# Mixture layers: the norm taken with tokens as partitions, the router on raw columns, one softmax for all tokens

## What is computed

```python
x = x + 0.5 * ffn(layernorm(x))          # two blocks of local attention and a gated MLP
x = x + ssm(layernorm(x))
x = x + 0.5 * ffn(layernorm(x))
x = x + 0.5 * mixture(layernorm(x))      # 8 experts, top 2
x = x + unit(layernorm(x))               # gated unit
x = x + 0.5 * mixture(layernorm(x))      # the same weights

def mixture(xf):
    probs = softmax(xf @ w_router)               # [tokens, 8]
    topk_w, topk_idx = top_k(probs, 2)           # not renormalised
    h = gelu(xf @ w1[e] + b1[e])                 # 128 -> 512
    return sum(topk_w * (h @ w2[e] + b2[e]))     # over the two experts
```

## Time and profile before

| | us |
|---|---|
| median of 3 runs (lowest, highest) | 1194.48 (1188.43, 1200.24) |
| the profiled execution, its own time | 1189.11 |
| its span | 1187.3 |
| mean granted TensorE clock | 0.926 of full |
| busy in the span: PE, DVE, ACT, POOL | 1012.3, 720.2, 688.2, 524.8 |
| DMA moved | 120.02 MB |

### The profile page before, as it was taken

One profiled execution on the slowest core, in us unless ns is written; L12 is line 12 of the kernel. 1 busy time (PEld: TensorE's weight loads), 2 busy tenths in 40 slices (PEclk: granted clock), 3 DMA queues, 4 the chain that ended last, 5 costly groups with the idle time before them and its releaser, 6 DMA issues.

```text
span 1187.3 us, 25908 instructions
## 1 busy us (share of the span) xinstructions
PE 1012.3 (85%) x9070; PEld 632.4 (53%) x9070; DVE 720.2 (61%) x1625; ACT 688.2 (58%) x1301; POOL 524.8 (44%) x405
## 2 busy tenths in 40 slices
PE   4788999999998876799999999999639968746995
PEld 1345555555555364355555555555339964325995
DVE  0577678777776653677776776876564423654441
ACT  2566686686673662676677667656316636623661
POOL 2664456556441542545444344433345530263451
PEclk9899999999999967999999999999759989857997
DMA  9895344455433600545444344432312240011223
GB/s 349 250 298 157 86 102 109 97 120 116 100 93 81 71 1 2 126 109 121 96 107 96 89 107 109 101 80 77 143 44 68 67 114 1 19 43 48 64 65 120
DMA packets 88511, 120.02 MB, mean 101 GB/s; under 512 B 20064, under 2 KB 72032, under 8 KB 87488
## 3 DMA queue, kind: packets, MB, share of 16 engines
q1 hardware_dynamic: 81824, 96.30, 33.8%
q0 software_dynamic: 6272, 20.44, 4.7%
q10 hardware_dynamic: 288, 1.63, 0.3%
HBM read 62.66 MB, written 22.11 MB: 71 GB/s over the span
## 4 chain that ended last, share of the span: by engine, by line
PE 65%; ACT 14%; issue 7%; DMA 6%; DVE 5%; POOL 1%; SPq 1%; ACTq 0%; DVEq 0%; POOLq 0%
PE banks L591 7%; PE banks L944 6%; PE banks L954 6%; PE banks L676 5%; PE banks L662 5%; PE banks L620 3%; PE banks L751 3%; PE banks L669 3%; PE banks L637 3%; PE banks L721 3%; PE banks L726 2%; PE banks L645 2%; DMA rstd<-arena 2%; ACT arena L1194 2%; ACT arena L1189 2%
## 5 line engine op out<-in xcount | busy, mean ns | idle before, releaser
L2041 POOL TENSOR_TENSOR arena<-arena 128x1024 f32<-128x1024 f32 x64 | 150.9, 2357 | 321.0 <-DVE arena L1644 318.7
L2030 POOL TENSOR_TENSOR arena<-arena 128x1024 f32<-128x1024 f32 x64 | 150.8, 2357 | 41.6 <-ACT arena L1189 41.6
L1636 DVE TENSOR_REDUCE arena<-banks 128x4 f32<-128x512 f32 x128 | 82.5, 686 | 93.5 <-PE banks L620 93.3
L1181 ACT ACTIVATE arena<-banks,arena 128x512 f32<-128x512 f32 x128 | 80.5, 679 | 93.6 <-PE banks L669 93.2
L591 PE MATMUL banks<-arena 128*128 128x512 f32 x256 | 128.6, 627 | 6.7 <-DVE arena L1563 5.9
L2020 POOL DMA_INDIRECT moe_outs<-arena x78 | 81.5, 1045 | 100.7 <-DVE arena L1882 88.6
L1386 ACT ACTIVATE arena<-banks,arena 128x128 f32<-128x128 f32 x312 | 89.0, 369 | 59.0 <-PE banks L944 58.9
L2013 POOL DMA_INDIRECT moe_rows<-arena x64 | 63.1, 986 | 118.5 <-DVE arena L1617 101.1
L1644 DVE TENSOR_TENSOR arena<-arena 128x1024 f32<-128x1024 f32 x64 | 78.1, 1220 | 28.4 <-DMA arena<-arena 28.4
L1194 ACT ACTIVATE arena<-banks 128x1024 f32<-128x1024 f32 x64 | 65.6, 1025 | 46.1 <-PE banks L591 45.1
L954 PE MATMUL banks<-arena 128*128 x624 | 87.5, 283 | 4.6 <-ACT arena L1386 4.4
(11 more groups left out here) (221 smaller groups left out, 1951.6 us busy)
## 6 DMA issues: line engine op xcount, KB each, us to landing
arena<-arena SPq DMA_DIRECT2D x256, 128.0 KB, 3.8
arena<-rstd SPq DMA_DIRECT2D x128, 256.0 KB, 4.3
moe_rows<-arena POOLq DMA_DIRECT2D x12, 903.0 KB, 6.6
arena<-moe_rows SPq DMA_DIRECT2D x78, 64.5 KB
arena<-in_rot SPq DMA_DIRECT2D x4, 1024.0 KB, 11.6
arena<-in_mw SPq DMA_DIRECT2D x2, 2048.0 KB, 10.8
arena<-moe_outs SPq DMA_DIRECT2D x16, 256.0 KB, 4.9
arena<-ssm_a SPq DMA_DIRECT2D x4, 512.0 KB, 6.6
```

The costliest lines, as they stand in the source:

```text
L1636: nc.vector.tensor_reduce(mx[:, e], by_row(bank[3 + e][:]), AX.X, ALU.max).then_inc(s_max, 1)
L2030: nc.gpsimd.tensor_tensor(TA[:, n % 2], RAW, ROTV[:, :, 0, c * C:(c + 1) * C], ALU.mult).then_inc(cos_done, 1)
L2041: nc.gpsimd.tensor_tensor(TA[:, n % 2], TA[:, n % 2], TB, ALU.add).then_inc(rot_sum, 1)
```

## The change

It alters both mixtures, nothing of their experts' loops but the source of the gates, and no DMA of SP.

- The weights of the router are centred once (`centred_router`: one product of 128x8 on PE, a copy on DVE into WRC, semaphore `wrc`). It stands on PE in the loop's last pass (s = 32) of the second ffn, ahead of the first piece of the mixture, and with it the wait for `moe_s_in` >= 48. DVE's copy stands behind `normalise(31)`.
- `token_rows` (PE): the rows come as four products of X's tile with the centring matrix, tokens as partitions; the products `centred` and `variance` over features, ACT's square and full-width ln and exp, DVE's multiply and the transposes go.
- `route` (PE): four router products from X and WRC. `pick` (DVE): the eight largest raw logits and their places straight from PSUM, the cast and the one-hot tables: 5 chained steps where `route` had 10.
- `moments` (DVE): four `bn_stats` and four `bn_aggr` of 128 columns, mean and variance of every token. `tokens` (ACT): ln and exp of 128x4, four copies of 128x128 with the row's scale, and a copy of the chunk from SBUF to SBUF.
- The gates: exp((logit - largest) * scale), its sum and reciprocal for all 16 tiles at once: `gates_start` behind `tile_map`, `gates_exp` on ACT, `gates_end` behind the weights of the first two tiles.
- The order of all pieces changes. In the tail of the ffn chunk 2 now comes ahead of `mlp_output(7)`; `rank(0, 0)` stands ahead of the last transposed scores; the second mixture's chunk 1 is made ahead of the unit's last silus.

The diff, cut to the new functions and the new orders:

```diff
+            def centred_router():
+                pe.wait_ge(moe_s_in, 48)
+                mm(bank[1][:, 0:NE], centre, WR, start=True, stop=True).then_inc(wrc, 1)
+
+            def route(moe, c):
+                pe.wait_ge(wrc, 2)
                 for t in range(TILES):
                     at = c * C + t * P
-                    last = mm(bank[MX_VAR[moe][c]][:, t * NE:(t + 1) * NE], YB[:, at:at + P], WR, start=True, stop=True)
+                    last = mm(bank[MX_RANK[moe][c]][:, t * NE:(t + 1) * NE], X[:, at:at + P], WRC, start=True, stop=True)
                 last.then_inc(router_mm, 1)
+
+            def token_rows(moe, c):
                 for t in range(TILES):
                     at = c * C + t * P
-                    last = nc.tensor.transpose(bank[MX_CEN[moe][c]][:, t * P:(t + 1) * P], YB[:, at:at + P], ident)
+                    last = mm(bank[MX_TOK[moe][c]][:, t * P:(t + 1) * P], X[:, at:at + P], centre, start=True, stop=True)
                 last.then_inc(xtok_mm, 1)
...
                     elif run:
                         pe.wait_ge(copied, 2 * n)
+                        pe.wait_ge(sq_done, n)
+                        centred_router()
                         pe.wait_ge(x_ffn, NCH + 1)
-                        centred(X, 0, MX_CEN[0][0])
+                        token_rows(0, 0)
...
                 if run:
-                    variance(mix, 0, MX_VAR[0][0])
+                    route(0, 0)
                 transpose_out(29, n - 3, s)
                 masks(31, n - 1)
                 values(30, n - 2, 0)
                 scores(31, n - 1)
                 values(30, n - 2, 1)
                 if run:
-                    pe.wait_ge(moe_s_in, 48)
-                    route(mix, 0, 0)
+                    rank(0, 0)
                 transpose_scores(31, n - 1)
                 hidden(6, s, 0)
...
                     pe.wait_ge(x_ffn, NCH + 2)
-                    centred(X, 1, MX_CEN[0][1])
+                    token_rows(0, 1)
+                    route(0, 1)
...
                 transpose_out(31, n - 1, s, 0)
-                if run:
-                    rank(0, 0)
                 output(7, s)
                 hidden(6, s, 1)
+                if run:
+                    rank(0, 1)
                 last_centred()
...
                 last_hidden(2)
-                if not run:
+                if run:
+                    pe.wait_ge(xtok_done, 3)
+                    pe.wait_ge(rank_dve, 2 * RANK_STEPS)
+                    pe.wait_ge(x_ffn, NCH + 3)
+                    token_rows(0, 2)
+                    route(0, 2)
...
                 mlp_output(7, s)
```

The unit's part on PE, `enter(c)` being `token_rows(1, c)` and `route(1, c)` behind their waits (x_unit; from chunk 1 on the first copy of the rows of the chunk before):

```diff
                 unit_centred(3)
-                mix_centred(0)
-                mix_variance(0)
                 down(1)
+                enter(0)
                 unit_variance(3)
-                route(mix, 1, 0)
                 up(2, range(3))
-                mix_centred(1)
                 rank(1, 0)
-                mix_variance(1)
+                enter(1)
                 up(2, range(3, 4))
                 up(3)
-                route(mix, 1, 1)
+                rank(1, 1)
                 down(2)
                 down(3)
-                rank(1, 1)
-                mix_centred(2)
-                mix_variance(2)
-                route(mix, 1, 2)
-                mix_centred(3)
+                enter(2)
+                enter(3)
                 rank(1, 2)
-                mix_variance(3)
-                route(mix, 1, 3)
                 rank(1, 3)
```

More of the change, by code:

```diff
@@ L1300, in ffn @@
                 if run:
-                    act.wait_ge(rs_out, 16 * n)
-                    act.wait_ge(unit_done, n)
-                    norm_root(mix, 1, MX_VAR[0][1])
+                    tokens(0, 1)
                 else:
@@ L1310, in ffn @@
                 if run:
-                    tokens(0, 1)
+                    tokens(0, 2)
                 else:
@@ L1598, in route @@
-                chained(TT(OH[:, tt], each, IDXF[:, tt, 0:2].unsqueeze(3).to_broadcast([P, TILES, 2, NE]), ALU.is_equal), route_dve)
-                chained(TT(MINE[:, tt], OH[:, tt, 0], OH[:, tt, 1], ALU.add), route_dve)
-                assert n[0] == ROUTE_STEPS * (k + 1)
+                for t in range(TILES):
+                    last = nc.vector.max(TOPL[:, c * TILES + t], part(moe, c, 0)[:, t])
+                chained(last, pick_dve)
+                for t in range(TILES):
+                    at = c * TILES + t
+                    last = nc.vector.max_index(TOPI[:, at], TOPL[:, at], part(moe, c, 0)[:, t])
@@ new lines, in pick, with moments @@
+                chained(last, pick_dve)
+                chained(nc.vector.tensor_copy(IDXF[:, tt], TOPI[:, tt]), pick_dve)
+                each = expert_id.unsqueeze(1).unsqueeze(1).to_broadcast([P, TILES, 2, NE])
+                chained(TT(OH[:, tt], each, IDXF[:, tt, 0:2].unsqueeze(3).to_broadcast([P, TILES, 2, NE]), ALU.is_equal), pick_dve)
+                chained(TT(MINE[:, tt], OH[:, tt, 0], OH[:, tt, 1], ALU.add), pick_dve)
+                assert n[0] == PICK_STEPS * (k + 1)
+            def moments(moe, c):
+                k = NCH * moe + c
+                dve.wait_ge(xtok_mm, k + 1)
+                for t in range(TILES):
+                    last = nc.vector.bn_stats(PART[:, c * TILES + t], bank[MX_TOK[moe][c]][:, t * P:(t + 1) * P])
+                last.then_inc(tok_dve, 1)
+                dve.wait_ge(tok_dve, 2 * k + 1)
+                for t in range(TILES):
+                    last = nc.vector.bn_aggr(MOMENT[:, c * TILES + t], PART[:, c * TILES + t])
+                last.then_inc(tok_dve, 1)
@@ L1751, in ffn @@
                 if run:
-                    norm_chunks(mix, first_plain, [0])
+                    dve.wait_ge(cos_done, n)
+                    centred_router()
+                    moments(0, 0)
                 maximum(n - 1)
                 subtract(n - 1)
+                if run:
+                    pick(0, 0)
                 divide(n - 2)
-                if run:
-                    dve.wait_ge(cos_done, n)
-                    route(0, 0)
                 divide(n - 1)
@@ L1763, in ffn @@
                 residual(7, gg - 1)
+                if run:
+                    pick(0, 1)
                 gate(6, gg - 2, 1)
+                if run:
+                    moments(0, 1)
                 gate(6, gg - 2, 2)
                 mlp_norm(7, gg - 1)
+                if run:
+                    rank(0, 1)
                 mlp_residual(6, gg - 2)
-                if run:
-                    norm_chunks(mix, first_plain, [1])
-                else:
+                if not run:
                     ssm_normed(0, 0)
@@ L1775, in ffn @@
                 if run:
-                    route(0, 1)
+                    pick(0, 2)
+                    moments(0, 2)
                 else:
@@ L1855, in mixture @@
                 if moe == 0:
-                    rank(0, 1)
-                    norm_chunks(norm0, first_plain, [2])
-                    route(0, 2)
                     rank(0, 2)
-                    norm_chunks(norm0, first_plain, [3])
-                    route(0, 3)
+                    pick(0, 3)
+                    moments(0, 3)
                     rank(0, 3)
                 tile_map()
+                gates_start(moe)
                 g0 = NT * moe
```

186 lines of the change are left out of this document (77 added, 109 removed).

## The result

The median after the change is 1211.16 us (4 runs, 1207.25 to 1215.84), beside 1191.86 for the kernel before (4 runs, 1188.43 to 1200.24): ratio 1.0153, 95% interval 1.0086 to 1.022. The changed kernel is slower by about 19 us; the forecast had said 8.3. In the profiled executions the time is 1211.06 against 1189.11 us, span 1209.3 against 1187.3.

The account below looks back on a forecast made before the run. The prediction took the chain of waits into POOL's 32nd row write, not PE's busy share, as the bound. First mixture +19.4 - 9.3 = +10.1 us, second -1.8: +8.3 on the median, 1203 us, range 1188 to 1214.

Parts of the forecast that it names:

- The likeliest case: Whole kernel: the forecast's own sum, +8.3 us on the median, 1203 us; chance 0.55.
- The wait of 8.8 us: First mixture, ahead of output(7): PE stands still at centred_router until the last moe_s_in load lands, 8.8 us.
- wait, router product and half clock: First mixture, at centred_router: PE's wait 8.8 us, the router product 0.2, half clock after the stall 2.1.
- Queueing behind route(0,0): Last attention steps: transpose_out(29), masks and values(30) queue behind route(0,0), so scores(31) begins 2.5 us later.
- rank and pick ahead of the transposed scores: Last attention steps: transposed scores wait for pick(0,0), and a second router set precedes the last transposes; 2.85 us.
- half clock again: Ahead of output(7): new idle times of about 3.4 and 4 us halve PE's clock; 3 us, at most about 8.
- Behind output(7): First mixture, output(7) to the 32nd write: POOL starts chunk 3 at +29.1, last write at +48.2 against 57.5; -9.3 us.
- Second mixture: Preparation to the 32nd write: silus 2.3 us late, but chunk 3 follows chunk 2 without a gap; -1.8 us.
- The gates, at nothing: Behind the map: DVE's work ends some 5 us before first rows land, so gates cost nothing; without that cover 1.5 us.
- The hidden wait: Rival at centred_router: loads land when PE arrives or the attention's tail has slack; -3.6, some 1191 us; chance 0.12.
- POOL's early chunks: Rival in both mixtures: the tail costs nothing and they end as soon as POOL can write; 1180 us; chance 0.05.
- Half clock spreads: Rival: PE stays at 1.2 GHz from 806 through output(7) and the MLP, delaying added(3); 1213 us; chance 0.23.

Follow-up runs that it names:

- before_wait: Kernel before plus only PE's wait for moe_s_in at the place where the change has it; 1202.29 us, ratio 1.012.
- tail_order: wait_later with PE's route(0,0) back behind values(30) and rank(0,0) back ahead of output(7); 1180.63 us, ratio 0.9947; repeated on another chip 1193.46 us, 1.0013.
- after_again: The changed kernel, unedited, run and profiled once more; 1205.98 us, ratio 1.0159.
- tail_late: tail_order with centred_router behind scores(31) on PE, its copy behind moments(0,0) on DVE; 1183.43 us, ratio 0.9976; repeated on another chip 1190.43 us, 0.9999.
- before_again: The kernel before, unchanged, profiled once more on a chip of its own; 1194.28 us, ratio 1.0025.
- wait_later: Changed kernel with centred_router and its wait moved behind the transposed scores of the loop's last pass; 1191.59 us, ratio 1.0038.
- own_bank: tail_late with bank 0 for chunk 3's rows in the second mixture, no wait for chunk 2's copy, rank(1,2) ahead of pick(1,3); 1176.88 us, ratio 0.9926.
- order_bank: tail_order with own_bank's edit in the second mixture, without tail_late's edit in the first; 1178.79 us, ratio 0.9914.
- silu_first: own_bank with ACT's tokens(1,1) behind silu(2) and silu(3); 1173.95 us, ratio 0.9899; repeated on another chip 1180.80 us, 0.9919.

## Why the forecast was right in kind and too small

The direction, the place of the wait and its cause were right, and 1211.16 lies inside the range, 1188 to 1214. That it does is partly luck: the upper end was there for a rival whose mechanism didn't happen (below). The likeliest case said 1203 and "within 1%", and the kernel is slower by 1.5%. By the forecast's own terms:

**The wait of 8.8 us**: 9.18 in this trace, 9.04 and 9.13 in two more. Right. PE arrived 1.96 us ahead of SP's `rstd` pair (before 2.12); the load took 4.6 us to land where the earlier trace rows has 4.2. The sum "wait, router product and half clock", 11.1, came to 12.0: from SP's `rstd` issue to the step's transposed scores (L679) it is 813.42 - 797.44 = 15.98 us, against 803.72 - 799.74 = 3.98 before. before_wait alone gives 11.9. By the Trainium skill's rule to issue a DMA early and wait on it late (DMA: Bandwidth & Descriptors, Rules for kernel authors) this place was wrong, and the runs agree: the same wait nine groups of instructions later costs 13.8 us less at output(7), and behind `scores(31)` PE doesn't wait for the load at all. The product needs only the first of the three loads, 4 KB, issued 1.07 us ahead of the last, and it landed in 3.5 us; with a semaphore of its own the wait would be shorter by 1.1 + 1.1 = 2.2 us, an estimate that no run tried.

**Queueing behind route(0,0), 2.5 us**: from the transposed scores (813.42) to `scores(31)` (822.08) it is 8.66 us, 4.21 before: 4.45 more. The list of what queues was right, each at full clock; the pieces ran at half: L571 1.87 us for eight where I counted 0.8.

**rank and pick ahead of the transposed scores, 2.85, and "half clock again", 3**: from `scores(31)` to output(7) 16.64 us against 10.29: 6.35 for these two. With the 1.95 left over from the term before, half clock again is 1.95 + 6.35 - 2.85 = 5.4 us, not 3; the rows bear that out, since from L571 to L736 the instructions take some 5 us longer, start to start, than at full clock. **This is the step that failed ahead of output(7)**: I priced the idle times of about 3.4 and 4 us rightly (3.25 and 3.78) and took for the clock behind them less than half of its upper bound (the 8 us of PE work in them once more). In all 22.8 for 19.4, inside its range of 16.4 to 24.4. tail_order took these idle times out: 4.85 us less at output(7).

**Behind output(7), -9.3 us**: -5.2, and -6.9 in after_again. **This is the second term that failed.** The forecast had POOL start its third chunk at +29.1. It starts at 871.57 - 838.72 = +32.9, and at +31.2 in after_again. `rank(0,1)` made PE wait for `pick(0,1)` as forecast, 1.67 us, and at half clock behind it the third chunk comes 1.4 us later. But this half clock is not a matter of the edit. The idle time is the same in all eleven traces of the new order, and the pieces behind it run at half clock in eight of them, the third chunk at +31.2 or more, and at full clock in three, the third chunk at +29.8, which is 0.7 from the forecast. tail_late and tail_late_again are one kernel and lie on either side:

```profile
827.13 1.02 PE L731 MATMUL banks<-arena 128*85 128x512 f32 x2
```

```profile
826.60 1.90 PE L731 MATMUL banks<-arena 128*85 128x512 f32 x2
```

The other 1.7 us of the first trace are pauses of 0.5 to 0.65 us between DVE's steps ahead of chunk 3's last sum, as before_again has them elsewhere. The 15 intervals of writes took 19.4 us for 19.1. The prices of the pieces stand: `moments` is 0.88 + 0.38 us (I took 1.3, from bounds 0.75 and 2.2), `tokens` 2.4 us (0.30 twice, 1.14 and 0.63 us).

**Second mixture, -1.8 us**: D to 32nd is 73.38 in after_again, +2.2, and 72.39 and 72.34 in wait_later and tail_late, whose second mixture is the same: +1.2. So the term is 3 to 4 us off. The silus are not the reason: the first starts 22.57 us behind D in after, 19.93 before, so 2.6 late where I had 2.3. (In after_again it is 23.95, since four `down` products behind an idle time of 2.04 us ran at half clock, 3.38 us for 1.99; that too happens in four of eleven traces, whatever the edit.) Against wait_later, POOL's third chunk starts 1.8 us later behind D than forecast. Half of that is one slip: between the end of `moments(1,2)` and `token_rows(1,3)` I counted 1.1 us for the first copy of the rows, but `tokens` has its ln and exp ahead of it, and it takes 2.0. And POOL's last 15 intervals took 20.3 us for 19.1 (last section). That chunk 3's rows run at half clock was forecast. The timelines of ACT, PE and POOL of after_again:

```profile
1040.15 1.84 ACT L1419 ACTIVATE arena<-banks,arena 128x512 f32<-128x512 f32 x3
```

```profile
1060.10 2.04 PE L577 MATMUL banks<-arena 128*128 128x128 f32 x8 [5.15 <-ACT arena L1168]
```

```profile
1069.26 0.97 POOL L2008 DMA_INDIRECT moe_rows<-arena  x1 [8.18 <-DVE arena L1606]
...
1089.58 0.97 POOL L2008 DMA_INDIRECT moe_rows<-arena  x1 [0.30 <-issue]
```

The forecast named the chain through bank 7 ("only then is bank 7 free for token_rows(1,3)") but priced it as a given; own_bank shows that to break it, with `rank(1,2)` moved up, is worth 7.7 us by the trace, more than any other term of this mixture. In the profiled execution of after, DVE's 7.4 us of idle time come on top (last section).

**The gates, at nothing**: the time from the second mixture's 32nd write to the end is 112.89 us in after and 115.62 in after_again, against 114.23 before. Nothing shows there, but no run took them out alone. The map, the gates and the diagonals are done in time, as forecast; what wasn't is that the diagonals, now ahead of POOL's last writes, come with slower writes, 1.2 us in the second mixture and 0.3 in the first.

**The sum.** By after_again: 23.3 - 6.9 = +16.4 in the first mixture for +10.1, and +3.0 between the two last writes (200.38 us against 197.36) for -1.8. Together 19.4, beside 19.1 between the medians of after_again and its before. That the two agree so closely is partly chance, since stretches that no edit touches vary by more (last section). Taken out one behind the other, the wait's place gives back 14.4 us by the medians (13.8 by the traces) and then the order of the last steps 11.0 (6.3 by the traces). Together that is 25.4, more than the 19.1 lost, so with both put right (tail_order) the change is 6.3 us faster than before on that chip, and level on another.

**The rivals.** The hidden wait and POOL's early chunks are refuted for this change. Of the second one's gain most comes once the pieces are placed otherwise: own_bank, with output(7) 1.4 us late, POOL's third chunk 7 us earlier behind output(7) than before and no gap behind the second chunk in the second mixture, is 9.3 us faster than its before; the rival had 14.3. "Half clock spreads", 18.5 us more, is the nearest to the 19.3 measured. Its mechanism as told isn't what happened: PE didn't stay at 1.2 GHz to output(7), whose eight products take 3.71 us as before; ahead of each next idle time the pieces ran at full clock again (L679 1.03 us, L647 0.69), and half clock came anew behind it.

## What to carry to other kernels

A wait added ahead of a dense chain costs its length and, on PE, the half clock behind it (here 9.1 + 2.8 us). Count the instructions behind every idle time that the new order makes and price them at the lower clock. Behind each idle time of 3.2 us and more shown here they ran at half clock, at the latest from the third group on; behind those of 1.7 and 2.0 us they did in some traces and not in others, in one and the same kernel, so there the price is a range and not a number. A new wait on a load belongs behind the last work that doesn't need the load; here the same wait costs 12 to 15 us or nothing that shows, by its place. And before an order is judged, ask which buffer makes two chunks wait for each other: one free bank (with `rank(1,2)` moved up) gave 6.6 us on one chip and 14.7 on another. order_bank and silu_first, the change with its pieces placed so, are 0.8 to 1.0% faster than the kernel before; what the saved arithmetic alone is worth no run shows.

## What the runs showed that I had not expected

- **DVE stands idle before a queue that the profile doesn't know.** The profiles of after and of the four kernels run together last have DVE idle for 1.75 to 8.21 us once or twice in the second mixture's preparation, beginning while POOL writes rows; the six other profiles of the new order, on two chips, have nothing of the kind. tail_order has it on one chip and not on another, so it isn't the code alone; chip and time of the runs changed together, so which of them it goes with isn't shown. tail_order's ratio differs by 0.0066 between the chips, some 8 us, beside 6.57 us of idle time in its second trace. Three of these profiles, and before_again on ACT, have another of about 2 us in the experts. What the queue is stays open, and no run took POOL's writes away from beside it. In the runs with the idle time the own bank is worth 14.7 us by the medians, in those without 6.6 (tail_late to own_bank); why wasn't tried.
- **POOL's writes are slower while DVE writes the diagonals.** They come 1.27 us apart, but 1.81 apart (1090.24, 1092.05, 1093.86 above) while DVE writes eight diagonal matrices, 1087.81 to 1092.72. All eleven traces of the new order have two such spacings there; before, the diagonals began with the last write (1072.98 and 1073.07), and its last spacings are 1.27 to 1.31 us. Single spacings of 1.6 to 1.8 us come elsewhere too, and no run moved the diagonals, so the cause is read from the timing alone. That is the 1.2 us by which the last row of writes was longer than forecast.
- **PE's clock gives stretches that no edit touched two lengths.** From the start of the combine to the first `down` it is 29.61 to 29.73 us in eight traces and 31.26 to 31.59 in five, 33.01 in one. In the first group the unit's first products behind the combine run at full clock, in the others at half, whatever the edit (the timelines of PE, before and after):

```profile
976.74 1.12 PE L991 MATMUL banks<-arena 128*128 128x512 f32 x2 [0.78 <-DVE arena L1827]
```

```profile
990.08 2.08 PE L994 MATMUL banks<-arena 128*128 128x512 f32 x2 [0.78 <-DVE arena L1826]
```

Before has the one length and before_wait, whose unit is the same, the other. The experts, from the first mixture's 32nd write to the combine, take 94.54 to 100.64 us (96.47 and 100.44 in two traces of before), and the layers ahead of the ruler end at 795.85 to 803.59; no cause of these was looked for. So a difference between two single profiles says nothing by itself below 3 us in such a stretch, or below some 6 us over the experts.
